# A two-layer graph kernel on one core: preparation laid over 128 partitions, the first chunk table formed on the chip, the first loads moved to SyncE

## The reference

```python
# layer 0: attention over the incoming edges, then a feed-forward block
q, k, v = X @ Wq, X @ Wk, X @ Wv                       # 8 heads of 16
scores = einsum('ehd,ehd->eh', q[dst], k[src]) / sqrt(16)
ex = exp(scores - segment_max(scores, dst)[dst])
alpha = ex / (segment_sum(ex, dst)[dst] + 1e-9)
h1 = layer_norm(X + segment_sum(alpha * v[src], dst) @ W0)
x = layernorm(x + layer_norm(h1 + relu(h1 @ fc1_w + fc1_b) @ fc2_w + fc2_b))
# layer 1: messages over the first and the second half of the edges
h_in  = segment_sum(relu(concat(x[src], ea, req) @ W1f + b1f) @ W2f + b2f, dst)   # first half
h_out = the same with W1b, b1b, W2b, b2b                                          # second half
out = layernorm(x + relu(((1 + eps) * x + h_in + h_out) @ Wu + bu))
```

## Time and profile before

| | us |
|---|---|
| median of three runs (2341.87, 2346.10, 2345.27) | 2345.27 |
| span of the profiled execution, first to last instruction | 2343.1 |
| preparation, until the first gather | 117.6 |
| edge stage of layer 0, first to last gather | 117.6 to 1102.7 |
| edge stage of layer 1, first to last gather | 1340.2 to 2317.7 |

### The profile page before, as it was taken

How to read it: one execution, slowest core, us unless ns; L and a number is a source line. 1 busy time by engine, 2 the same in 40 slices (tenths; PEclk the granted TensorE clock), 3 DMA queues, 4 the chain that set the end, 5 groups by cost and what they waited for, 6 DMA issues and landing times.

```text
span 2343.1 us, 31906 instructions
## 1 busy us (share of the span) xinstructions
PE 1413.2 (60%) x7352; PEld 1104.8 (47%) x7353; DVE 1443.4 (62%) x2963; ACT 743.4 (32%) x1515; POOL 1594.1 (68%) x1668
## 2 busy tenths in 40 slices
PE   5234656555555556556688566666666666566665
PEld 3134655455455455555566444444444444344443
DVE  2246978877877777778477444554554554544544
ACT  2143434344344334334367311111111111111111
POOL 4077777777777777776433277777777777777774
PEclk9657877778777778777799777777777777777777
DMA  4478555555555555554000122222222222222221
GB/s 167 126 177 279 175 155 163 166 155 163 166 154 159 169 156 154 173 156 146 22 33 35 48 60 63 65 63 62 65 64 63 65 64 65 63 64 65 63 63 45
DMA packets 149172, 255.38 MB, mean 109 GB/s; under 512 B 74828, under 2 KB 100096, under 8 KB 149004
## 3 DMA queue, kind: packets, MB, share of 16 engines
q0 software_dynamic: 65072, 160.39, 24.2%
q1 hardware_dynamic: 82194, 92.81, 12.8%
q10 hardware_dynamic: 1870, 1.78, 0.2%
HBM read 233.19 MB, written 28.04 MB: 111 GB/s over the span
## 4 chain that ended last, share of the span: by engine, by line
POOL 60%; issue 22%; DMA 5%; DVE 5%; PE 4%; ACT 2%; POOLq 1%; another core or an unknown queue 1%; DVEq 0%; SPq 0%; ACTq 0%; PEldq 0%
POOL arena L720 31%; POOL arena L663 28%; DMA kvq_tab<-arena 3%; DMA arena<-kvq_tab,arena 1%; ACT arena L876 1%; PE ps L1083 1%; DVE arena L1526 1%; DMA xs<-in_x_dram 1%; DVE arena L1516 0%; PE ps L1119 0%; DVE arena L1471 0%; PE ps L1124 0%; PE ps L1171 0%; DVE arena L1551 0%
## 5 line engine op out<-in xcount | busy, mean ns | idle before, releaser
L663 POOL DMA_INDIRECT arena<-kvq_tab,arena x784 | 747.5, 953 | 265.9 <-issue 264.9
L720 POOL DMA_INDIRECT arena<-y_tab,arena x784 | 739.8, 944 | 252.4 <-issue 238.6
L1083 PE MATMUL ps<-arena 128*128 128x136 f32 x1568 | 316.1, 388 | 413.4 <-DVE arena L1471 413.4
L1083 PEld LDWEIGHTS ps<-arena 128*128 128x128 f32 x1568 | 306.4, 292 | 428.5 <-issue 428.5
L953 ACT ACTIVATE arena<-arena 128x512 f32<-128x512 f32 x224 | 123.3, 572 | 795.3 <-DVE arena L1607 795.3
L1607 DVE TENSOR_TENSOR arena<-ps,arena 128x512 f32<-128x512 f32 x224 | 134.7, 621 | 353.8 <-DMA arena<-y_tab,arena 344.6
L1233 PEld LDWEIGHTS ps<-arena 128*128 128x128 f32 x1568 | 265.1, 244 | 163.7 <-ACT arena L953 95.8
L1233 PE MATMUL ps<-arena 128*128 128x128 f32 x1568 | 286.4, 336 | 30.3 <-ACT arena L953 29.6
L1220 PE MATMUL ps<-w1blk,eaT 113*128 x456 | 253.3, 643 | 0.6 <-ACT eaT L948 0.6
L1417 DVE TENSOR_TENSOR arena<-ps,arena 128x512 f32<-128x512 f32 x224 | 137.9, 616 | 170.6 <-DMA arena<-kvq_tab,arena 168.5
L1059 PE MATMUL ps<-arena 128*128 128x128 f32 x1596 | 212.1, 287 | 41.7 <-ACT arena L812 26.8
(11 more groups left out here) (247 smaller groups left out, 1949.6 us busy)
## 6 DMA issues: line engine op xcount, KB each, us to landing
arena<-d SPq DMA_DIRECT2D x58, 897.0 KB, 4.9
arena<-kvq_tab,arena POOLq DMA_INDIRECT x784, 2.7
arena<-y_tab,arena POOLq DMA_INDIRECT x784, 2.5
arena<-ea SPq DMA_DIRECT2D x60, 112.0 KB, 2.0
ea<-in_edge_attr_dram SPq DMA_DIRECT2D x2, 3125.0 KB, 19.1
y_tab<-arena SPq DMA_DIRECT2D x10, 625.0 KB
kvq_tab<-arena SPq DMA_DIRECT2D x6, 937.5 KB
arena<-kvq_tab SPq DMA_DIRECT2D x59, 64.0 KB
```

Of the source, the lines that this page charges most:

```text
L663: g.indirect_dma_start(kv_s[:, r, t, :], None, kvq_tab.rearrange("n (a d) -> (n a) d", a=3), bass.IndirectOffsetOnAxis(ap=v3(idx, RING)[:, ...
L720: g.indirect_dma_start(yg_s[:, r, t, :], None, y_tab, bass.IndirectOffsetOnAxis(ap=v3(idx1, RING)[:, r, t:t + 1], axis=0)).then_inc(m_g[r] ...
L1083: last = mm(sums, hot_s[:, u, t, :], contrib_s[:, u, t * RW:(t + 1) * RW], start=(t == 0), stop=(t == G - 1))
```

## The change

The nodes are laid over all 128 partitions in the preparation, 49 (PT) a partition, in seven groups of seven tiles (PG). 127 partitions are full, the last one holds 27 rows (LAST), and DVE clears the rest. x is loaded in pieces of 112 partitions, 15 and 1. `kvq_tab` keeps its rows; the padding moves behind row 6272. All seven stores are SP's, into three slots. Results use five PSUM banks instead of six, since one holds the marks and the table. The edge lists use 80 partitions x 625 instead of 125 x 400.

The marks of both layers are read by ACT from `dst` itself, onto one partition, converted by DVE and spread over the partitions by a product with ones on TensorE. `chunk_table(0)` moves ahead of the conversions and of all copies on DVE; its result is turned by TensorE (`turn_table`, behind the second group's products) and copied by DVE in its third group. The second layer's table still goes through DRAM. The loads that ACT issued before the edge stage stand on SP behind the fifth store. Since the stage over the nodes still wants 125 x 50, SP loads x again in `late_loads(0)`.

```diff
-EP, EQ = 125, 400
+EP, EQ = 80, 625
+PT, PG = 49, 7
+PGROUPS = PT // PG
+PN = P * PT
+FULL = N // PT
+LAST = N - FULL * PT
+assert PT == PG * PGROUPS and FULL == P - 1
+WHOLE = 112
+TAB = PN + W
...
-        xT = carve(2 * GRP * P, 0)
-        KVR = 5
-        BY_POOL = (2, 4, 6, 8)
-        slots = [(0, 0), (1, 0), (3, 0), (2, 0), (4, 0), (0, 1), (3, 1), (1, 1), (4, 1), (2, 1)]
-        kvst = carve(KVR * GRP * QKV)
+        xT = carve(2 * PG * P, 0)
+        KVR = 3
+        slots = [(i % KVR, i // KVR) for i in range(PGROUPS)]
+        uses = [len(range(k, PGROUPS, KVR)) for k in range(KVR)]
+        kvst = carve(KVR * PG * QKV)
         srci = carve(2 * EQ).bitcast(I32)
         srcb = carve(2 * EQ).bitcast(I32)
...
-            x_rows = x.rearrange("(p t) d -> p t d", t=TILES)
-            span = 2 * GRP
-            for k in range(GROUPS // 2):
-                sp.dma_start(v3(xs[:, :], TILES)[0:NT, k * span:(k + 1) * span, :], x_rows[:, k * span:(k + 1) * span, :]).then_inc(s_x[k], 16)
-                if k == 0:
-                    sp.dma_start(v3(xs[:, :], TILES)[NT:P, :, :], x_rows[0:P - NT, :, :]).then_inc(s_xr, 16)
...
+            x3 = v3(xs[:, 0:PT * D], PT)
+            x_rows = x[0:FULL * PT, :].rearrange("(p t) d -> p t d", t=PT)
+            sp.dma_start(x3[0:WHOLE, 0:PG, :], x_rows[0:WHOLE, 0:PG, :]).then_inc(s_x[0], 16)
+            sp.dma_start(x3[WHOLE:FULL, 0:PG, :], x_rows[WHOLE:FULL, 0:PG, :]).then_inc(s_xb[0], 16)
+            sp.dma_start(x3[FULL:P, 0:LAST, :], x[FULL * PT:N, :].rearrange("(p t) d -> p t d", p=1)).then_inc(s_xb[0], 16)
+            sp.wait_ge(s_xz, 1)
+            sp.dma_start(x3[0:WHOLE, PG:3 * PG, :], x_rows[0:WHOLE, PG:3 * PG, :]).then_inc(s_x[1], 16)
+            sp.dma_start(x3[WHOLE:FULL, PG:PT, :], x_rows[WHOLE:FULL, PG:PT, :]).then_inc(s_xb[1], 16)
+            for k in (2, 3):
+                sp.dma_start(x3[0:WHOLE, (2 * k - 1) * PG:(2 * k + 1) * PG, :],
+                             x_rows[0:WHOLE, (2 * k - 1) * PG:(2 * k + 1) * PG, :]).then_inc(s_x[k], 16)
...
                 u = slots[i][0]
-                sp.wait_ge(s_ca, acts(i * GRP + GRP - 1))
-                sp.wait_ge(s_cv, vecs(i * GRP + GRP - 1))
-                sp.dma_start(by_row(kvq_tab, i * GRP, GRP)[:, :, 0:QKV], kvst_s[0:NT, u, :, :]).then_inc(s_kvo[u], 16)
...
+                sp.wait_ge(s_ca, acts(i * PG + PG - 1))
+                sp.wait_ge(s_cv, vecs(i * PG + PG - 1))
+                sp.dma_start(by_row(kvq_tab, i * PG, PG), kvst_s[:, u, :, :]).then_inc(s_kvo[u], 16)
...
-            for i in range(GROUPS):
-                if i not in BY_POOL:
-                    store_rows(i)
-            sp.wait_ge(s_tabi[0], 32)
+            def first_loads():
+                sp.wait_ge(s_tab0, 2)
+                sp.wait_ge(s_arr, 16 * 3)
+                sp.wait_ge(s_d0, 48)
+                for c in range(RING):
+                    off = sp.value_load(tab_sb[0][0:1, ds(c, 1)], min_val=0, max_val=NB * CH)
+                    sp.dma_start(v3(idx, RING)[:, c, :], by_lane(i0[ds(off, CH)])).then_inc(l_ix[c], 16)
+                    if c == 0:
+                        sp.dma_start(dstb, d0[ds(off, DB)].rearrange("(a n) -> a n", a=1).to_broadcast([P, DB])).then_inc(l_db, 16)
+                    if c < 2:
+                        sp.dma_start(v3(dcol, RING)[:, c, 0:G], by_lane(d0[ds(off, CH)])).then_inc(l_ld[c], 16)
+                        sp.dma_start(v3(dcol, RING)[:, c, G:DC], by_lane(d0[ds(off + G, CH)])[:, 0:2]).then_inc(l_ld[c], 16)
+
+            for i in range(PGROUPS):
+                store_rows(i)
+                if i == 4:
+                    first_loads()
+            sp.wait_ge(s_tab0, 2)
...
-                    sp.dma_start(tabs[1], tbe[0:TE, 0:5].bitcast(I32)).then_inc(s_tabo[1], 16)
-                    sp.dma_start(negs[1].rearrange("(p c) -> p c", c=1), tbe[0:TE, 5:6]).then_inc(s_tabo[1], 16)
-                    sp.dma_start(ways, tbe[0:TE, 7:9]).then_inc(s_tabo[1], 16)
+                    sp.dma_start(tab1, tbe[0:TE, 0:5].bitcast(I32)).then_inc(s_tabo, 16)
+                    sp.dma_start(neg1.rearrange("(p c) -> p c", c=1), tbe[0:TE, 5:6]).then_inc(s_tabo, 16)
+                    sp.dma_start(ways, tbe[0:TE, 7:9]).then_inc(s_tabo, 16)
+                    node_rows = x.rearrange("(p t) d -> p t d", t=TILES)
+                    sp.dma_start(v3(xs[:, :], TILES)[0:NT, :, :], node_rows).then_inc(s_xr, 16)
+                    sp.dma_start(v3(xs[:, :], TILES)[NT:P, :, :], node_rows[0:P - NT, :, :]).then_inc(s_xr, 16)
...
-            def store_rows(i):
-                pool.wait_ge(s_ca, acts(i * GRP + GRP - 1))
-                pool.wait_ge(s_cv, vecs(i * GRP + GRP - 1))
-                pool.dma_start(by_row(kvq_tab, i * GRP, GRP)[:, :, 0:QKV], kvst_s[0:NT, slots[i][0], :, :]).then_inc(s_kvo[slots[i][0]], 16)
...
-            store_rows(2)
-            pool.wait_ge(s_d0, 48)
-            pool.dma_start(firsts[0].rearrange("(b c) -> b c", c=1), marks(d0[1:1 + NB * CH]), allow_slow_non_contiguous=True).then_inc(s_first[0], 16)
...
-            store_rows(4)
-            pool.wait_ge(s_first[0], 16)
-            spread(0)
...
-            store_rows(6)
...
-            pool.wait_ge(s_ea, 16 * 10)
-            pool.dma_start(firsts[1].rearrange("(b c) -> b c", c=1), marks(d1), allow_slow_non_contiguous=True).then_inc(s_first[1], 16)
-            pool.wait_ge(s_tab, 1)
-            pool.dma_start(tabs[0], tbe[0:TE, 0:5].bitcast(I32)).then_inc(s_tabo[0], 16)
-            pool.dma_start(negs[0].rearrange("(p c) -> p c", c=1), tbe[0:TE, 5:6]).then_inc(s_tabo[0], 16)
-            store_rows(8)
-            pool.wait_ge(s_first[1], 16)
-            spread(1)
-            pool.wait_ge(s_tabo[0], 32)
-            pool.dma_start(tab_sb[0][:, :], tabs[0].rearrange("(a e) f -> a (e f)", a=1)).then_inc(s_tabi[0], 16)
-            pool.dma_start(nj[0][:, :], negs[0].rearrange("(a e) -> a e", a=1).to_broadcast([P, TE])).then_inc(s_tabi[0], 16)
...
+            pool.wait_ge(s_tab0, 2)
...
+            def load_marks(at, start, n):
+                starts = dst[start:start + n * CH].rearrange("(b c) -> c b", c=CH)[0:1, :]
+                act.dma_start(marki[:, at:at + n], starts, allow_slow_non_contiguous=True).then_inc(s_mark, 16)
...
+            load_marks(0, 0, NB - 1)
+            load_mark(NB - 1, (NB - 1) * CH)
+            load_marks(NB, 0, BLK - 1)
+            load_mark(NB + BLK - 1, (BLK - 1) * CH)
+            load_marks(NB + BLK, HALF, BLK - 1)
+            load_mark(2 * NB - 1, HALF + (BLK - 1) * CH)
             act.dma_start(v3(dsti, 2)[0:EP], dst_halves).then_inc(s_dst, 16)
             act.dma_start(v3(srci, 2)[0:EP], src_halves).then_inc(s_dst, 16)
...
-            def first_loads():
-                by_lane = lambda a: a.rearrange("(p g) -> p g", g=G)
-                act.wait_ge(s_tabi[0], 32)
...
-            first_loads()
...
-            pe.wait_ge(s_wq, 2)
+            pe.wait_ge(s_wq, 1)
+            pe.wait_ge(s_markf, 1)
+            mm(bank(7)[:, 0:2 * NB], ones[0:1, :], markf).then_inc(s_markb, 1)
...
-                pe.wait_ge(s_x[i // 2], 16)
+                pe.wait_ge(s_x[(i + 1) // 2], 16)
+                if i == 0:
+                    pe.wait_ge(s_xb[0], 32)
+                if i == 1:
+                    pe.wait_ge(s_xb[1], 16)
...
+            def turn_table():
+                pe.wait_ge(s_tab, 1)
+                for f in range(2):
+                    tp(bank(7)[0:1, (f + 1) * TE:(f + 2) * TE], tbe[0:TE, f:f + 1], ident[0:TE, 0:TE])
+                mm(bank(7)[:, 3 * TE:4 * TE], ones[0:TE, :], diag[0:TE, :]).then_inc(s_turn, 1)
...
+            pe.wait_ge(s_wq, 2)
...
-                for t in range(GRP):
-                    j = i * GRP + t
-                    if j >= 6:
-                        pe.wait_ge(*((s_cv, vecs(j - 6)) if j % 2 else (s_ca, acts(j - 6))))
...
+                for t in range(PG):
+                    j = i * PG + t
+                    if j >= 5:
+                        pe.wait_ge(*((s_ca, acts(j - 5)) if j % 2 else (s_cv, vecs(j - 5))))
+                    mm(bank(2 + j % 5)[:, 0:QKV], v3(xT, 2)[:, i % 2, t * P:(t + 1) * P], wqkv[:, :]).then_inc(s_kv, 1)
+                if i == 1:
+                    turn_table()
...
+            v.memset(v3(xs[:, 0:PT * D], PT)[96:P, LAST:PT, :], 0.0).then_inc(s_xz, 1)
             v.memset(ps[:, :], 0.0).then_inc(s_wq, 1)
+            dve.wait_ge(s_mark, 16 * 6)
+            v.tensor_copy(markf, marki).then_inc(s_markf, 1)
...
-            dve.wait_ge(s_dst, 32)
...
-                dve.wait_ge(s_first[l], 32)
+                link(v.tensor_copy(first[:, 0:NB], markb[:, l * NB:(l + 1) * NB]))
...
-                    ts(entry[:, 0:1], which, float(CH), None, ALU.mult)
-                    v.tensor_copy(entry[:, 1:2], off)
-                    ts(entry[:, 2:5], tbe[0:rows_, 10:13], 0.0, None, ALU.mult)
+                    ts(tbe[0:rows_, 0:1], which, float(CH), None, ALU.mult)
```

(24 more changed lines are left out.)

144 lines of the change are left out of this document (61 added, 83 removed).

## The result

The changed kernel takes 2320.06 us (median of four runs, 2317.31 to 2325.16) where the kernel before takes 2345.68 on the same chip: a ratio of 0.9894, with a 95% interval of 0.9879 to 0.9909. The forecast was 2292.7 with a range of 2284 to 2306. The direction is right, but half of the expected gain of 52.6 us is missing. The profiled execution has a span of 2318.4 us against 2343.1.

A forecast was written before the change was run, and what follows sets the result against it. The first gather's start was taken as the bound, held back by the spread of the preparation's transfers. Span 2343.1 - 54.6 (earlier first gather) + 2 (reload) = 2290.5, plus 2.2 around it: 2292.7 us, range 2284 to 2306.

The forecast's parts named there:

- What bounds the kernel: Whole kernel: the first gather's start, 117.56 us, sets the end; preparation ending 1 us earlier ends the program 1 us earlier.
- Spread: Preparation's transfers: 128, 112 and 80 partitions use 16 engines instead of five, at 340 GB/s, slow end 260.
- Start and VectorE's list: Start of preparation: first multiplications at about 14 us, VectorE's first copy at about 19.5 after table and list conversions.
- Tiles: Preparation's tile groups: 5.28 us per group of 7, last tile copied at 53 us, three staging slots just enough.
- First loads: Loads on SP behind the fifth store: 7.0 us of issue, holding the sixth store until 49.6; cost 0 or 0.5 us.
- End: End of preparation: last store issued at 53.2, landed by 60 to 61, first gather at 63, gaining 54.6 us.
- Reload of x: First edge stage: SP's second load of x, about 32 us beside gathers, costs 2 us, bounds 0 and 15.
- The delay replaces waits: First edge stage: later loads and attribute copy come 14 us later, replacing waits like those 8.55 us, not adding.
- The gathers themselves should pass: First edge stage: gathers get past the reload, one per 1.3 us, as a row of x takes 1 us.
- Rival 1: Preparation's stores: DRAM writes are the bound at 260 GB/s, first gather at 70 to 73, time 2301; chance 0.16.
- Rival 2: First edge stage: reload and attribute copy add up, lateness 14 less 2.8 margin reaches GpSimd, time 2302; chance 0.14.
- Rival 3: Preparation's stores: SP's hardware queue does not spread, five engines carry them, first gather 116.5, time 2354; chance 0.04.

The follow-up runs named there:

- e8: e3 with each of the seven stores split into 125 partitions and 3: 2344.02 us, ratio 1.0000 to the kernel before.
- e9: e7 with SyncE's signal that the preparation is over placed ahead of its first loads: 2291.91 us, ratio 0.9770 to the kernel before.
- e1: The changed kernel without most of its reload of x (49 of 50 rows per partition left out, wrong values): 2293.16 us, ratio 0.9772 to the kernel before.
- e13: The changed kernel with its reload of x issued by ScalarE at the end of its chunk 0 pass, not by SyncE: 2317.39 us, ratio 0.9886.
- e14: The changed kernel with the edge-attribute copy moved behind SyncE's last loads of the first edge stage, reload kept in place: 2316.90 us, ratio 0.9885.
- e4: The kernel before with only the reload of x added, at the same place as in the changed kernel: 2374.63 us, ratio 1.0116.
- e3: The changed kernel with the reload split into 112, 13 and 3 partitions and moved behind SyncE's last loads of the first edge stage: 2296.12 us, ratio 0.9780.
- e5: e3 with SyncE's first loads moved behind the seventh store: 2297.94 us, ratio 0.9797 to the kernel before.
- e7: e3 with SyncE's first loads behind the seventh store and VectorE's list conversion behind its first group's copies: 2292.89 us, ratio 0.9776.
- e10: e3 with VectorE's list conversion behind its first group's copies and SyncE's first loads behind the fourth store: 2297.66 us, ratio 0.9790.

## Why the prediction was wrong, by its own steps

*What bounds the kernel*: right. The first gather's start set the time, and the 24.7 us by which the span fell are the 47.6 less the 23.0 of the stage, to 0.1.

*Spread*: right, and without it nothing is gained (e8). The rate was under-estimated: 430 GB/s in the last stores, not 340. The Trainium skill's page "DMA: Bandwidth & Descriptors" (section "Why a DMA increments its semaphore by 16 and not by 1") says that a transfer runs on the largest number of engines up to 16 that divides the slowest dimension of both its sides, which is 16 for 128 and 5 for 125. The trace agrees, with shares of 1.04 and, in e8, 0.32. The same page (section "Where 436 GB/s comes from") says that a core's limit to HBM, 358 GB/s, binds such transfers, and that 435 is the ceiling of the ports; it has the 358 as half of what two cores share, and here one core runs. The measurement decides: the stores moved 430 GB/s, over the first figure and just under the second.

*Start and VectorE's list*: **this term was mis-sized, by 6 us of the 7 that are missing before the first gather.** The forecast had the marks by 7.7 us; VectorE waited for them until 10.97, 2.77 us. It had the lists there when the table was done; they landed at 23.0, 3.4 us after VectorE was ready. Both are transfers of the first microseconds, where the sum took 340 GB/s. The stretch 0 to 10 had 180 GB/s at a share of 0.81 and 10 to 20 had 211 at 0.92, so the engines were busy and moved little; that the small rows of the marks do this is only argued. The table itself took from 13.5 to 19.6, 6.1 for the 5.9 forecast. The first copy at 25.6 is past the 25 that the prediction had named as a sign of being wrong.

*Tiles*: right. A group takes 5.28 us, and no copy waited for one of the three slots. 25.6 in place of 19.5 at the first copy gave 59.9 in place of 53 at the last.

*First loads*: 7.0 us to issue, as counted, but they held the sixth store to 59.3, not 49.6, as they began at 52.2. The two stores had landed 7.2 us after the last issue, where 7 to 8 were forecast. A last store alone landed in 4.9 (e9), so the bunching cost some 2 us, not 0.5, seen in one profiled run of each. In the changed kernel the faster stores hid that.

*End*: last issue to first gather, 9.6 us, forecast 9.8. The forecast's own terms add up to more: 53.2, 7.0, 2 and 2.36 are 64.6, not 63. So it was right by luck in part: 430 GB/s in place of 340 made up for the 1.6 us that its sum had dropped, and for the bunching.

*Reload of x*: **the step that failed.** It was priced at 2 us, and the stage became 23.0 longer, more than the 10 that the prediction had named as a sign of being wrong. Its length was under-estimated: 24 to 32 us expected on five engines, 40 seen. That SyncE's later loads would come late was right. "The delay replaces waits" is what was wrong: VectorE's waits are 27.6 us longer than in e1, 19.7 of them for those loads, and the stage is 24.2 longer. "The gathers themselves should pass" was wrong by less: 35.0 us of waits for them, where e1 has 27.1 without the reload. The step put a load over all engines behind the reload on SyncE's queue alone; e13 shows such a load waiting for the five engines from another queue too. And it took SyncE's issue for free, which stood 18.1 and 12.0 us. The rows that bounded it were of the attribute copy, which moved 6.4 MB in some 20 us, more than twice what five engines carried in any run here.

*Rivals.* Rival 1 (the stores drain at 260 GB/s) is refuted, with 430. Rival 2 had the right place and sign, the reload's delay going into GpSimd, but the wrong mechanism and half the size: 11 us by a sum with the copy, where e14 shows 19 without it. The reload's bound of 15 us was too low, since e1 and e4 put the price at 24 to 29. Rival 3 didn't occur, but e8 is its case, and its first gather of 116.5 is close to the 119.1 measured.

What stays open: why SyncE's issue is held 12 to 30 us during the reload (its length is shown, its cause isn't: the mean share was down to 0.57 while it lasted), and what the six mark loads cost at the start, which no run isolated.

## What to carry to other kernels

Before a transfer is put beside a stream of small ones, count the engines that it uses: a transfer over all engines can then wait for those (e13). 3.2 MB on five engines cost 23 to 29 us in the middle of a conveyor. At its end, over all engines, it cost nothing that the runs tell from leaving it out (e3 and e1); on five engines there, VectorE had to wait for it. When a stage is shortened at its front, the next item on the list of the queue that signals can become the end (e5, e7): look at what that queue still has to issue, and signal first. In e9 that brought the earliest first gather of all runs, but only 1 us in the median, within the scatter.

## What the runs showed of the hardware

- Stores over 128 partitions moved 430 GB/s, more than any stretch shown of the kernel before (378).
- Stores over 125 partitions and 3 moved 123 to 127 GB/s at a share of 0.31 to 0.33 (e8).
- Of a load over 128 partitions issued beside the reload, 88 packets began within 7 us and the other 40, as many as five engines carry, 18 to 30 us after the issue, though the reload was on another issuer's queue (e13).
- The issue of a small load, 0.35 us otherwise, took 1.0 to 1.5 us in e10 at a share of 0.93 to 1.01, and 18.1, 12.0 and 30.0 us beside the reload, even where the reload was on another issuer's queue. At a share of 0.96 to 0.98 in the changed kernel it took 0.34 to 0.39.
- In the first 10 us the engines were busy to 0.81 at only 180 GB/s.
